# Shared expert's parts moved two rounds forward in the written-out orders of a mixture-of-experts kernel, and half of the one-hot rows moved behind the next group's first maximum

## What is computed

```python
attn_in = tanh(x @ W1 + b1); scores = attn_in @ v
p = softmax(where(mask, scores[:, None, :], NEG_INF))
pooled = einsum('bjl,bld->bjd', p, x) / cnt
...
scores = softmax(pooled @ wg.T)                     # 32 experts, 8 groups of 4
keep 4 groups by their maximum, then the top 4 experts of those
pos = (cumsum(one_hot(idx)) * one_hot(idx)).sum(-1) - 1; keep = pos < 640
buf_tok = token at slot expert * 640 + pos
out = (silu(xe @ w1) * (xe @ w3)) @ w2              # xe: gathered rows, per expert
z = (silu(pooled @ sw1) * (pooled @ sw3)) @ sw2     # shared expert
x = x + y + z
```

## Time and profile before

| | us |
|---|---|
| median of three runs | 1539.36 |
| lowest, highest run | 1530.76, 1539.44 |
| the profiled execution | 1537.86 |
| its span in the trace | 1536.1 |

### The profile page before, as it was taken

The page is one execution under the profiler, slowest core; times in us unless marked ns, Lnnn a source line. Parts: engine busy times, 40 slices in busy tenths (PEclk is TensorE's granted clock), DMA queues, the critical chain, the costliest instruction groups (busy, mean ns, idle before and its releaser), DMA issues.

```text
span 1536.1 us, 27264 instructions
## 1 busy us (share of the span) xinstructions
PE 1402.7 (91%) x9777; PEld 1219.8 (79%) x9777; DVE 1030.4 (67%) x2418; ACT 897.8 (58%) x2092; POOL 654.4 (43%) x624
## 2 busy tenths in 40 slices
PE   7987899999999998789998999998729999999996
PEld 5765799999999997568776776776618998998996
DVE  2998567767777775678887887885435556555552
ACT  5775345545555552268887787788626456455452
POOL 0222344434443414455556666643434445345333
PEclk9997899999999999999999999999759999999998
DMA  5421256666655633557576587575422343234212
GB/s 170 138 83 37 64 152 179 174 163 184 175 169 168 178 98 106 100 96 132 122 141 134 100 131 143 99 123 90 123 85 55 87 108 89 47 92 97 41 22 28
DMA packets 134326, 173.59 MB, mean 113 GB/s; under 512 B 21461, under 2 KB 106272, under 8 KB 134192
## 3 DMA queue, kind: packets, MB, share of 16 engines
q1 hardware_dynamic: 106032, 119.89, 30.4%
q0 software_dynamic: 28160, 51.96, 17.7%
HBM read 107.28 MB, written 42.08 MB: 97 GB/s over the span
## 4 chain that ended last, share of the span: by engine, by line
PE 72%; DVE 9%; issue 6%; DMA 6%; ACT 3%; another core or an unknown queue 2%; POOL 2%; SPq 1%; POOLq 0%; DVEq 0%; ACTq 0%
PE banks L929 45%; PE banks L1437 5%; DMA xe<-pooled,idx 4%; PE banks L1480 4%; PE banks L1533 3%; PE banks L991 3%; PE banks L451 2%; PE banks L1493 2%; PE banks L1454 1%; PE banks L1495 1%; PE banks L1909 1%; PE banks L571 1%; DVE row_at L516 1%; PE banks L1452 1%
## 5 line engine op out<-in xcount | busy, mean ns | idle before, releaser
L929 PE MATMUL banks<-hi_x,hi_w 128*128 128x320 f32 (+1 forms) x832 | 290.7, 349 | 12.1 <-DVE hidden L964 5.2
L929 PE MATMUL banks<-lo_x,hi_w 128*128 128x320 f32 (+1 forms) x832 | 288.1, 346 | 0.0
L929 PE MATMUL banks<-hi_x,lo_w 128*128 128x320 f32 (+1 forms) x832 | 287.6, 346 | 0.0
L929 PE MATMUL banks<-hi_w,hi_h 128*128 128x256 f32 x896 | 261.1, 291 | 2.5 <-DVE X L1018 2.1
L870 POOL DMA_INDIRECT xe<-pooled,idx x160 | 159.2, 995 | 237.4 <-DVE hidden L964 104.3
L929 PE MATMUL banks<-lo_w,hi_h 128*128 128x256 f32 x896 | 253.8, 283 | 0.0
L929 PE MATMUL banks<-hi_w,lo_h 128*128 128x256 f32 x896 | 253.7, 283 | 0.0
L1894 POOL DMA_INDIRECT out<-X,tab x64 | 106.1, 1658 | 190.7 <-DVE X L1997 176.1
L1584 ACT ACTIVATE PN<-banks,smax 128x256 f32<-128x256 f32 (+1 forms) x512 | 180.0, 442 | 12.6 <-DVE smax L1690 12.6
L1410 POOL DMA_INDIRECT got<-done,slot x128 | 126.6, 989 | 133.9 <-DVE smax L1690 70.4
L929 PEld LDWEIGHTS banks<-hi_x,hi_w 128*128 128x128 f32 x832 | 159.9, 192 | 27.3 <-issue 11.0
(11 more groups left out here) (187 smaller groups left out, 2950.7 us busy)
## 6 DMA issues: line engine op xcount, KB each, us to landing
w<-in_L_ffn_w SPq DMA_DIRECT2D x96, 256.0 KB
done<-res SPq DMA_DIRECT2D x32, 640.0 KB
BIG<-in_L_ffn_W SPq DMA_DIRECT2D x16, 1024.0 KB
QS<-parts_qk SPq DMA_DIRECT2D x96, 128.0 KB
KS<-parts_qk SPq DMA_DIRECT2D x96, 128.0 KB
mask<-in_c_masks SPq DMA_DIRECT2D x16, 257.0 KB, 2.8
pooled<-XF SPq DMA_DIRECT2D x16, 256.0 KB, 3.2
WS<-in_L_cond_W SPq DMA_DIRECT2D x16, 256.0 KB
```

The source lines that it names most:

```text
L929: last = e.matmul(o, a[i], b[j], start=start and k == 0, stop=stop and k == 2, skip_group_check=True)
```

## The change

It does two things. First, all shared expert's entries (`split_x`, `up`, `split_h`, `down`) get offsets two larger in the PE, DVE and ACT tables: part 0 is begun two rounds earlier. Second, the `lane` step of a group's second half moves on DVE from behind `choose` 3 to behind the next group's `logits` and `rank`, and on ACT `token` 2 moves behind `logits`. `dve_found`, which stood ahead of the last `split_h`, now stands behind the whole stage.

```diff
     PE_ROUND0 = (
...
-        ("up", -5, 1), ("mix", 3, 0), ("find", 0, 2), ("mix", 3, 1), ("down", -6, 0), ("find", 0, 3),
+        ("up", -3, 1), ("mix", 3, 0), ("find", 0, 2), ("mix", 3, 1), ("down", -4, 0), ("find", 0, 3),
...
     DVE_ROUND0 = (
-        ("split_x", -2, 0), ("scores", 6, 0), ("up", -3, 0), ("logits", 4), ("rank", 3),
+        ("split_x", 0, 0), ("scores", 6, 0), ("up", -1, 0), ("logits", 4), ("rank", 3), ("lane", 2, 1),
...
     ACT_ROUND0 = (
...
-        ("turn_back", 2, 0), ("turn_back", 2, 1), ("token", 0, 0), ("token", 0, 1), ("up", -5, 0), ("token", 0, 2),
+        ("turn_back", 2, 0), ("turn_back", 2, 1), ("token", 0, 0), ("token", 0, 1), ("up", -3, 0),
...
             elif step == "split_h":
-                if (g, *d) == (NSH - 1, 1):
-                    dve_found(e)
                 dve_split_h(e, g, *d)
             elif step == "down":
                 dve_down(e, g, *d)
+        dve_found(e)
```

More of the change, by code:

```diff
@@ L406, in _build @@
         ("logits", 2), ("rank", 1), ("find", 0, 1), ("hidden", 4, 1), ("hidden", 5, 0), ("turn_p", 3, 1),
-        ("up", -5, 1), ("mix", 3, 0), ("find", 0, 2), ("mix", 3, 1), ("down", -6, 0), ("find", 0, 3),
-        ("turn", 5, 1), ("turn", 6, 0), ("up", -4, 0), ("turn_back", 3, 0), ("turn_back", 3, 1),
-        ("scores", 4, 1), ("down", -6, 1), ("scores", 5, 0), ("turn_p", 4, 0), ("find", 1, 0))
+        ("up", -3, 1), ("mix", 3, 0), ("find", 0, 2), ("mix", 3, 1), ("down", -4, 0), ("find", 0, 3),
@@ L410, in _build @@
+        ("turn", 5, 1), ("turn", 6, 0), ("up", -2, 0), ("turn_back", 3, 0), ("turn_back", 3, 1),
+        ("scores", 4, 1), ("down", -4, 1), ("scores", 5, 0), ("turn_p", 4, 0), ("find", 1, 0))
     DVE_ROUND0 = (
-        ("split_x", -2, 0), ("scores", 6, 0), ("up", -3, 0), ("logits", 4), ("rank", 3),
-        ("norm", 5, 1), ("choose", 4, 0), ("split_x", -2, 1), ("down", -5, 1), ("slots", 3),
-        ("choose", 4, 1), ("split_h", -3, 0), ("up", -3, 1), ("lane", 3, 0), ("choose", 4, 2), ("choose", 4, 3),
@@ L414, in _build @@
-        ("lane", 3, 1), ("scores", 6, 1), ("down", -4, 0), ("norm", 6, 0), ("split_h", -3, 1), ("choose", 4, 4))
+        ("split_x", 0, 0), ("scores", 6, 0), ("up", -1, 0), ("logits", 4), ("rank", 3), ("lane", 2, 1),
+        ("norm", 5, 1), ("choose", 4, 0), ("split_x", 0, 1), ("down", -3, 1), ("slots", 3),
+        ("choose", 4, 1), ("split_h", -1, 0), ("up", -1, 1), ("lane", 3, 0), ("choose", 4, 2), ("choose", 4, 3),
+        ("scores", 6, 1), ("down", -2, 0), ("norm", 6, 0), ("split_h", -1, 1), ("choose", 4, 4))
@@ L415, in _build @@
     ACT_ROUND0 = (
-        ("mix", 2, 1), ("split_x", -4, 1), ("turn", 4, 1), ("split_h", -6, 1), ("turn", 5, 0),
-        ("turn_back", 2, 0), ("turn_back", 2, 1), ("token", 0, 0), ("token", 0, 1), ("up", -5, 0), ("token", 0, 2),
-        ("split_h", -5, 0), ("weigh", 3, 1), ("turn_p", 3, 0), ("logits", 2), ("token", 0, 3), ("hidden", 4, 1),
-        ("split_x", -3, 0), ("up", -5, 1), ("weigh", 4, 0), ("turn_p", 3, 1), ("hidden", 5, 0), ("mix", 3, 0))
+        ("mix", 2, 1), ("split_x", -2, 1), ("turn", 4, 1), ("split_h", -4, 1), ("turn", 5, 0),
@@ L420, in _build @@
+        ("turn_back", 2, 0), ("turn_back", 2, 1), ("token", 0, 0), ("token", 0, 1), ("up", -3, 0),
+        ("split_h", -3, 0), ("weigh", 3, 1), ("turn_p", 3, 0), ("logits", 2), ("token", 0, 2), ("token", 0, 3), ("hidden", 4, 1),
+        ("split_x", -1, 0), ("up", -3, 1), ("weigh", 4, 0), ("turn_p", 3, 1), ("hidden", 5, 0), ("mix", 3, 0))
     POOL_ROUND0 = (("count", 6), ("pick", 6))
```

## The result

| | before | after |
|---|---|---|
| median, us | 1539.4 (four runs, 1530.76 to 1540.77) | 1553.37 (four runs, 1551.41 to 1557.32) |
| the profiled execution | 1537.86 | 1551.41 |
| its span | 1536.1 | 1549.6 |
| `idx` written, in the trace | 167.09 | 182.21 |

The changed kernel is slower: the ratio is 1.0111, with a 95% interval of 1.0087 to 1.0134. The forecast was 1541 us, range 1531 to 1550, with 0.95 for no difference of over 1%. The time lies above the range; the ratio's interval leaves open whether the loss is over 1%.

What follows compares the result with a forecast made beforehand. It took the first stage, gated by `idx` and with DVE almost always busy, as what the change affects. Its steps put `idx` at 170.6, 3.5 later than 167.1; on 1537.86 that gives 1541.4, forecast 1541 us, range 1531 to 1550.

Steps and rivals of the forecast that it cites:

- the measure: End of the first stage: the time `idx` is written, against 167.1, with the rest of the span moving with it.
- the nine table loads after the first: ACT in the first stage: six more loads than before, six of the nine on the chain, 1.3 us each.
- the waits of DVE for the exponentials: Ahead of `gs` of groups 5 and 6: DVE waits 1 to 3 us for ACT's exponentials.
- `hit` to `idx`: The first stage's tail, behind the last `hit`: 13.3 us against 22.0 before; the sign allowed 12 to 15.
- the last `gs` to `hit`: Group 7's choice on DVE: 10.4 us in both kernels, so the last `hit` ends at 157.3.
- "right" list: First-stage signs of a correct forecast: nine loads, DVE's waits, `gs` 7 some 12 us later, `hit` to `idx` 12 to 15, `idx` near 170.
- ups of 5 us ahead of turn_back: PE in the first stage: sign of a wrong forecast, half clock, where the forecast had ups of 2.8 us.
- Group 5 to group 6: Round between these groups' `gs`, by ACT and PE in turn: 21.6 us against 16.2 before, `gs` 6 at 129.7.
- a rival with 0.13: PE drops to 1.2 GHz while waiting; three ups on the chain cost 2.4 more each, +7.2: 1548.6 us; chance 0.13.
- Group 6 to group 7: Round between these groups' `gs`, PE's second down waiting for DVE's add: 17.2 us against 16.3, `gs` 7 at 146.9.
- Up to `gs` 4: First groups on DVE: added work +2.5, filled waits -0.6, `row_at` -0.8; together +1.1, `gs` 4 at 88.9.
- Group 4 to 5: Round between these groups' `gs`, silu ahead of `weigh`: 19.15 us against 14.4 before, `gs` 5 at 108.1.

Runs made afterwards that it cites:

- experiment 3: The changed kernel with part 2's first `hi_x` moved behind `turn_p` on ACT; ratio 1.0066 to the kernel before.
- experiment 12: experiment 3 plus five useless PE products in each of two waits ahead of `turn_p`, before the wait for the bank; ratio 1.0089 to the kernel before.
- experiment 6: The kernel before with second-half one-hot rows behind the next group's first `choose` piece and tokens 2 and 3 behind `weigh`; ratio 0.9982.
- 10: The changed kernel with tanh for silu in the first stage's shared parts and part 2's first `hi_x` behind `turn_p`; ratio 1.0023 to the kernel before.
- experiment 4: The changed kernel with tanh instead of silu in the first stage's three shared parts, another function without table switches; ratio 1.0033 to the kernel before.

## Why the prediction was wrong

Right in kind: the measure (the span moved with `idx`, and `idx` to the first turn of rows kept its 8.8 us), the nine table loads after the first at 1.28 us each, the waits of DVE for the exponentials, `hit` to `idx` (forecast 12 to 15, measured 14.7) and the last `gs` to `hit` (10.4). Loads and waits on ACT were named as what hurts. Of the "right" list, `gs` 7 (22 later instead of 12) and `idx` fell, and one sign of being wrong came true: ups of 5 us ahead of turn_back.

The steps that failed:

- "Group 5 to group 6 ... ACT in turn: two tokens 1.3, tanh 0.4, hi_x 0.5". 21.6 forecast, 27.5 measured. ACT's queue was summed as busy time, and the `hi_x` of part 2 has a wait on PE's ups of part 0, through a buffer shared by every second part. Measured 3.60 us of idle time; taking this `hi_x` from ahead of the silu brought the interval to 21.6 (experiment 3), some 1.5 of it through the clock. This is the largest miss, and it could have been read from `act_split_x` in the kernel.
- The ups were priced at 2.8 us throughout. Two took 4.99 and 5.09, behind waits of 3.07 and 3.64; the `mix` behind the wait of 3.66 took 2.92 instead of 1.93. I had this as a rival with 0.13 and gave "its gaps shrink" as the reason against it. My own sum had DVE wait some 3 us in a round and never asked how long PE waits there. Forecast and rival were not two worlds: the waits that the forecast counted are what brought the half clock. It cost less than the 7.2 I gave it alone, as far as it could be measured: 1.7 between groups 6 and 7 (experiment 12), and some 1.5 between 5 and 6, in the `mix` and the up behind the wait of 3.66 (experiment 3). What the slow first up adds through the `hi_x` wait was not measured by itself.
- "Group 6 to group 7 ... that add stands behind `choose` 3": I let DVE's add set the round, 17.2. Measured 21.0, and PE set it: from 134.66 to logits at 151.85 it had next to no gap, with an up at half clock and one of 2.77 in it. The maximum stood 17.5 behind `gs` 6 instead of 14.8. The other 1.0 is `row_at` behind it, which took 1.83. The forecast followed only one of the queues ahead of the maximum. (The forecast's terms add up to 16.9 where it has 17.1, which changes little.)
- Up to `gs` 4: `row_at` beside `pick` was bounded by 0.82 and 1.35, the trace's most. It took 1.89. A bound taken from one pair of neighbours doesn't hold for another. Three of them at 1.89, where the sum had the middle of 0.82 and 1.35, are 2.4 us; `gs` 4 came 2.1 later than forecast.
- Group 4 to 5 was 1.5 shorter than forecast, and the tail 1.4 longer.

The page of the Trainium skill, "ScalarE: Activation LUTs", section "What ACT_TABLE_LOAD costs", prices a switch to another table set at some 2.66 us. ACT's timeline of the changed kernel does not agree:

```profile
128.84 1.28 ACT L954 ACT_TABLE_LOAD   x1
130.13 0.60 ACT L954 ACTIVATE gate<-banks 128x512 f32<-128x512 f32 x1
```

A load takes 1.28 and the silu starts 1.29 behind its start, so a switch costs 1.3 us, as the earlier trace rows had it. By the page's figure the total would have come nearer, but not for its reason. The loads are worth 9 of the 15 us; their own length was in the forecast, the growth of the waits behind them was not.

The range erred as well. It was the forecast and the scatter of the runs, and each rival was priced alone. The losses here feed each other: a load makes PE wait, the wait brings the clock down, the slow up holds `hi_x`, and ACT's next load starts late.

## What to carry to other kernels

When a step is moved into an engine's queue, list every semaphore that it waits on, its buffer's last reader too, before adding up durations; and place a second table's function where the exponentials of no group stand behind it. When a sum of steps contains waits on another engine, walk every queue of the round, TensorE's too, and price its products behind such a wait at both clocks. Work that moves from a tail with idle time into a round that is full is paid in the round; here, with no table loads on either side, `gs` 7 came 13.9 us later and the tail gave 7.5 back. Compare a stripped kernel with a base that is stripped the same way.

## What the runs showed of the hardware

DVE's fp16 `row_at` (128x1280) and POOL's operations on tensors slow each other by how they fall together: `row_at` 0.82 us alone, 1.35 beside `two` and `sel`, 1.89 beside `pick`; `two` 0.72 alone and 1.11, `sel` 0.45 alone and 0.92, `pick` 1.27 alone (experiment 6) and 1.75. The rows look as if the two engines take turns: in the changed kernel `lane_at` ends at 89.00, `pick` at 90.14 and `row_at` at 90.82, within 0.3 of what the lengths alone of `pick` and `row_at`, one behind the other, would give. It can also fall out the other way: in experiment 6 `pick` at 149.83 took 3.11 us beside three DVE operations, of which `row_at` kept its 0.83. The sum over `row_at` and the three POOL operations is 4.65 us in the kernel before and 4.81 in the changed one, against 3.26 where each is alone; which of them is on the chain differs.

Behind waits of TensorE of 2.1 to 3.7 us in the rounds from group 5 to 7 of the changed kernel and of experiments 3, 10 and 12 the granted clock fell to 1.2 GHz, and 12 products of 512 columns took 3.3 to 5.1 us instead of 2.8; behind 1.3 and 1.9 us (experiment 4) it did not. The length of one wait doesn't decide alone: eight products took 3.55 us behind a wait of 1.04 and 3.67 behind 1.47 (experiment 4, at 87.59), but 1.94 behind 1.46 in the changed kernel (at 87.49). Useless products in the wait kept 2.4 GHz behind it (experiment 12, 126.57). They gained time only where TensorE itself was next on the chain.
